# A two-layer macaron block on one core: expert biases moved out of the expert matmuls into one gate-weighted matmul per batch, second mixture in phases of 3, 3 and 2 batches, second phase's scatters close together

## What is computed

```python
x = x + 0.5 * L0_ffn(layernorm(x))     # first mixture: 8 experts, the 2 best per token
x = x + L0_attn(layernorm(x))          # 16 heads of 8, causal
x = x + 0.5 * L0_ffn(layernorm(x))     # second mixture, same weights
x = x + 0.5 * L1_ffn(layernorm(x))     # 128x128 matmul of quantized blocks, plus bias
x = x + L1_attn(layernorm(x))          # a gated scan along the sequence, then a gated FFN of 384
x = x + 0.5 * L1_ffn(layernorm(x))

# in L0_ffn, for each expert:
h = relu(x @ w1 + b1)
y = h @ w2 + b2
acc = acc + y * c[..., None]           # c: the token's gate for this expert, 0 for 6 of 8
```

## Time and profile before

| | us |
|---|---|
| median of 3 runs | 953.89 |
| lowest and highest | 950.68, 956.58 |
| the profiled execution | 953.64 |
| its span, first to last instruction | 951.9 |

### The profile page before, as it was taken

The page is one execution under the profiler, slowest core; times in us unless marked ns, Lnnn a source line. Parts: engine busy times, 40 slices in busy tenths (PEclk is TensorE's granted clock), DMA queues, the critical chain, the costliest instruction groups (busy, mean ns, idle before and its releaser), DMA issues.

```text
span 951.9 us, 23220 instructions
## 1 busy us (share of the span) xinstructions
PE 843.4 (89%) x7513; PEld 612.7 (64%) x7513; DVE 612.6 (64%) x1906; ACT 551.4 (58%) x1230; POOL 662.0 (70%) x846
## 2 busy tenths in 40 slices
PE   6379899989999999999999999999987998756894
PEld 3279798837665765665566655559965997344563
DVE  7620255674687977788979777865435335588775
ACT  4345444365568666675776667575763557735752
POOL 3789785998864378597734986971899874886432
PEclk8679899999999999998999999999999999878897
DMA  8878576736553434533443543325533771101000
GB/s 310 293 228 249 166 207 193 224 108 182 168 162 94 119 118 144 143 105 103 122 135 107 146 141 98 112 65 156 156 95 97 219 210 56 28 26 33 1 12 33
DMA packets 116280, 127.65 MB, mean 134 GB/s; under 512 B 14779, under 2 KB 84667, under 8 KB 116038
## 3 DMA queue, kind: packets, MB, share of 16 engines
q1 hardware_dynamic: 107974, 109.38, 39.4%
q0 software_dynamic: 8192, 16.79, 5.9%
HBM read 85.35 MB, written 40.39 MB: 132 GB/s over the span
## 4 chain that ended last, share of the span: by engine, by line
PE 41%; POOL 29%; DVE 15%; issue 7%; ACT 5%; DMA 2%; POOLq 0%; DVEq 0%; ACTq 0%
PE bank L801 38%; POOL z_scratch L1700 9%; POOL small L1691 9%; POOL yg L1713 4%; PE bank L813 4%; DVE sm_m L1324 3%; ACT P L1575 2%; POOL P L1735 2%; POOL sm_f L1675 1%; DMA yg<-y_scratch,pos 1%; DVE xs L1265 1%; POOL sm_p L1675 1%; DVE sm_f L1146 1%; POOL xs L1771 1%; ACT P L1488 1%
## 5 line engine op out<-in xcount | busy, mean ns | idle before, releaser
L1324 DVE TENSOR_REDUCE sm_m<-bank 128x4 f32<-128x512 f32 (+2 forms) x320 | 204.5, 683 | 37.8 <-PE bank L801 37.0
L1575 ACT ACTIVATE P<-bank 128x512 f32<-128x512 f32 x320 | 175.9, 601 | 60.1 <-PE bank L801 55.6
L801 PE MATMUL bank<-w2r,hb 128*128 x1360 | 188.0, 282 | 0.0
L801 PE MATMUL bank<-zt,wt 128*128 128x128 f32 x1360 | 182.9, 285 | 4.6 <-ACT zt L1518 2.9
L801 PEld LDWEIGHTS bank<-zt,wt 128*128 128x128 f32 x1360 | 167.3, 197 | 17.9 <-ACT P L1575 5.0
L1735 POOL TENSOR_SCALAR_AFFINE_SELECT P<-P 128x256 f32<-128x256 f32 (+1 forms) x320 | 115.5, 377 | 90.5 <-ACT P L1575 86.8
L801 PEld LDWEIGHTS bank<-w2r,hb 128*128 128x128 f32 x1360 | 165.6, 192 | 3.4 <-issue 1.6
L1700 POOL DMA_INDIRECT z_scratch<-zb,pos x128 | 134.2, 1048 | 45.7 <-issue 25.8
L1534 ACT ACTIVATE hb<-bank 128x512 f32<-128x512 f32 x170 | 101.3, 597 | 90.9 <-PE bank L801 90.5
L1691 POOL TENSOR_TENSOR small<-small 128x4 f32<-128x4 f32 x140 | 148.3, 1059 | 6.9 <-DVE pos L1247 3.6
L1713 POOL DMA_INDIRECT yg<-y_scratch,pos x128 | 130.8, 1022 | 23.9 <-issue 20.2
(11 more groups left out here) (221 smaller groups left out, 1362.5 us busy)
## 6 DMA issues: line engine op xcount, KB each, us to landing
wt<-w_scratch SPq DMA_DIRECT2D x170, 256.0 KB
zin<-z_scratch SPq DMA_DIRECT2D x82, 128.0 KB
y_scratch<-yt SPq DMA_DIRECT2D x82, 128.0 KB
q_scratch<-qpart SPq DMA_DIRECT2D x48, 128.0 KB
k_scratch<-kpart SPq DMA_DIRECT2D x48, 128.0 KB
Ks<-k_scratch SPq DMA_DIRECT2D x64, 96.0 KB
Qs<-q_scratch SPq DMA_DIRECT2D x64, 96.0 KB
z_scratch<-P SPq DMA_DIRECT2D x6, 512.0 KB, 7.0
```

Source lines behind the costliest of these rows:

```text
L801: return e.matmul(o, lhs, rhs, start=start, stop=stop, **kw)
L1324: e.tensor_reduce(to, of, AX.X, ALU.max, negate=True).then_inc(*d_max.step(i, f"m{s_}"))
L1575: e.activation(P[:, (2 * i + s_) % PR, :], shared("scor", i, 0, s_), ACT.Exp, scale=SCALE).then_inc(*a_sc.step(i, f"e{s_}"))
```

## The change

1. The expert bias leaves `res`: no `bank<-bias,ones` matmul in a block (170 fewer), and `bias` holds only the bias of L1_ffn.
2. A new stage `shift` for each of the 16 units adds `0.5 * sum(gate * b2)` to `xs` directly. DVE makes the 32 products of one-hot and gate (two operations) and their sum, PE transposes the result (128x32 to 32x128), ACT copies it out of PSUM, PE multiplies it with a block-diagonal `b2d` (32x512, a new input), and DVE adds the 512-wide result to `xs`. `comb` of a unit waits for this addition; for the second mixture the addition waits for the attention of the batch. `prep` of the next phase also waits until `share` has been computed, since it overwrites the one-hots.
3. `ORDER`: the second mixture's phases are batches 0,1,2 / 3,4,5 / 6,7 instead of 0,1 / 2,3,4 / 5,6,7. The number of blocks stays 170, in 31, 31 and 23 instead of 23, 31 and 31.
4. `apart` gives `ROWS_CLOSE` to the second phase's scatters too. Over the whole program 29 of the 140 pauses go.
5. The planner ends differently: 6 passes instead of 8, and the best pass's priorities, changed by a table `FAVOUR`, are used for one more forward pass.

The core of the diff:

```diff
-ORDER = [of(1, 0, 1), of(1, 2, 3, 4), of(1, 5, 6, 7), of(2, 0, 1), of(2, 2, 3, 4), of(2, 5, 6, 7)]
+ORDER = [of(1, 0, 1), of(1, 2, 3, 4), of(1, 5, 6, 7), of(2, 0, 1, 2), of(2, 3, 4, 5), of(2, 6, 7)]
...
-    "bias": ("D1.4 D1.4 D1.0 D1.4",
+    "bias": ("D0.4 D0.3 D0.3 D0.3",
...
-    "res": ("P1 P1+0.2 A0.3+0.15 S0.5+4.5",
+    "res": ("P0.9 P0.9+0.2 A0.3+0.15 S0.5+4.5",
...
+    "shift": ("D0.6+0.15 P0.12+0.2 A0.26+0.15 P0.45+0.2 D0.6+0.15",
+            [(1, 2), (3, 4)], 1),
...
+    if stage == "shift":
+        return [[("prep", u, 9), ("shift", u - GR, 1)], [], [("shift", u - 1, 3)], [("begin", 0, 4)],
+                [("heads", USES[u][1], 3)] if USES[u][0] == 2 else []][k]
     if stage == "comb":
-        return [("res", PAIR[last_block(OF_TILE[u])][0], 3), ("comb", u - YR, 2)] if k == 0 else []
+        return [[("res", PAIR[last_block(OF_TILE[u])][0], 3), ("comb", u - YR, 2)], [], [("shift", u // 4, 4)]][k]
...
-    return ROWS_CLOSE if stage == "scat" and OF_TILE[u] == 0 else ROWS_APART
+    return ROWS_CLOSE if stage == "scat" and OF_TILE[u] < 2 else ROWS_APART
...
+FAVOUR = {
+    "prep": {3: 5, 4: 25, 5: 25},
...
-    rows, bank_of, _ = found
+    rows, bank_of, _ = forward(plan, queues, before, {x: v + favour(x[0], x[1]) for x, v in found[1].items()})
...
+            def shift(q):
+                o = take("shift", q, 1, a_shift.at(q, "t"))
+                w.wait_ge(l_first, 64)
+                w.wait_ge(*d_shift.at(q, "g"))
+                e.transpose(o[0:32, 0:128], share[:, q % GR, 0, :], ident[:, :]).then_inc(*t_shift.step(q, "t"))
+                yield
+                o = take("shift", q, 3, d_shift.at(q, "x"))
+                w.wait_ge(l_b2, 16)
+                w.wait_ge(*a_shift.at(q, "t"))
+                mm(o, sharet[:, :], b2d[:, :], True, True).then_inc(*t_shift.step(q, "y"))
+                yield
...
-                        mm(y, ones[:, :], bias[:, bass.DynSlice(at, 128)], j == 0, False, skip_group_check=True)
                         for c in range(NC):
-                            t = mm(y, hb[u % HB][:, c, :], w2[:, bass.DynSlice(at * 4 + 128 * c, 128)], False, c == NC - 1,
+                            t = mm(y, hb[u % HB][:, c, :], w2[:, bass.DynSlice(at * 4 + 128 * c, 128)], j == 0 and c == 0, c == NC - 1,
                                    skip_group_check=True)
...
+                for k, name in enumerate("ab"):
+                    e.tensor_tensor(parts[:, k, :, :], oh[:, k, T, :], gate[:, b, k, :].unsqueeze(2).to_broadcast([128, 4, 8]), ALU.mult
+                                    ).then_inc(*d_shift.step(q, name))
+                w.wait_ge(*d_shift.at(q, "b"))
+                e.tensor_tensor(share[:, q % GR, 0, :], share[:, q % GR, 0, :], share[:, q % GR, 1, :], ALU.add
+                                ).then_inc(*d_shift.step(q, "g"))
+                yield
+                w.wait_ge(*t_shift.at(q, "y"))
+                x_ready(w, q)
+                x = xs[:, b, :, :]
+                e.tensor_tensor(x, x, blocks(shared("shift", q, 3)), ALU.add).then_inc(*d_shift.step(q, "x"))
+                yield
```

More of the change, by code:

```diff
@@ L75 @@
 SMALL = 128 + 8 * TILES
[L76 removed]
+BIAS = 128
 ZR = 5
@@ L94 @@
 YR = 5
+GR = 3
 QR = 3
@@ L273, in network @@
 def network():
-    counts = {"begin": 1, "first": 1, "xload": NB - 2, "zero": 1, "fill": 1, "late": 1, "later": 1, "sload": NE, "split": NE, "wquant": 1, "prep": 2 * NB, "route": PHASES, "scat": NTILE,
+    counts = {"begin": 1, "first": 1, "xload": NB - 2, "zero": 1, "fill": 1, "late": 1, "later": 1, "sload": NE, "split": NE, "wquant": 1, "prep": 2 * NB, "shift": 2 * NB, "route": PHASES, "scat": NTILE,
               "bias": 1,
@@ L536, in build @@
         rt = sb("rt", [128, 6, 8 * TILES])
+        share, sharet = sb("share", [128, GR, 2, 32]), sb("sharet", [32, 128])
+        b2d = sb("b2d", [32, S])
         rs = sb("rs", [128, 24 + KB + 2 * TILES + 8 * EB])
@@ L1477, in vector_program @@
             begin()
-            follow("D", {"first": first, "bias": bias_parts, "prep": prep, "route": route, "comb": comb, "proj": proj,
+            follow("D", {"first": first, "bias": bias_parts, "prep": prep, "shift": shifted, "route": route, "comb": comb, "proj": proj,
                          "maxi": maxi, "mrow": mrow, "val": val, "heads": heads, "wquant": wquant, "mxa": mx(0), "mxb": mx(1),
@@ L1505, in prep, with shift @@
                 e.activation(sm_[:, 140:144], sm_[:, 136:140], ACT.Exp).then_inc(*f.step(q, "e"))
+                yield
+            def shift(q):
+                w.wait_ge(*t_shift.at(q, "t"))
+                if q:
+                    w.wait_ge(*t_shift.at(q - 1, "y"))
+                e.activation(sharet[:, :], shared("shift", q, 1)[0:32, 0:128], ACT.Copy).then_inc(*a_shift.step(q, "t"))
                 yield
@@ L1855 @@
     w2 = g["L0_ffn_W2"].reshape(NE, NC, 128, D).transpose(2, 0, 1, 3).reshape(128, NE, 512)
-    bias = np.concatenate([g["L0_ffn_b2"].reshape(-1), g["L1_ffn_bias"]])
+    b2d = np.zeros((4, NE, 4, D), np.float32)
+    for j in range(4):
+        b2d[j, :, j, :] = g["L0_ffn_b2"]
     arrays = {
```

56 lines of the change are left out of this document (42 added, 14 removed), and 2 rows, old and new, of the table STAGES.

## The result

The changed kernel takes **968.31 us** (median), the kernel before 955.24 beside it: ratio 1.0131, 95% interval 1.0106 to 1.0157. Each of the two medians is over four executions with one far longer among them (2748.91 and 1878.18 us); the ratio leaves these two out, and the medians without them are 966.82 and 953.89. Forecast were 946.5 us and 928 to 961. By the ratio the change makes the kernel 12.5 us slower, and the result lies 6 to 7 us above the range. The profiled execution took 969.79 us.

A forecast was written before the change was run, and what follows sets the result against it. The prediction took PE as the bound from 53 to 797 us, with DVE close behind mid-kernel. Its terms, -8.2 - 3.9 - 4 - 6 + 12 + 3 = -7.1, took the profiled 953.64 us to 946.5 us, range 928 to 961.

The forecast's parts named there:

- What bounds the kernel: From 53 to 797 us PE is the bound, so work taken off it there is paid unless DVE takes over.
- The bias matmul (-18.9): In the blocks, 170 bias matmuls fewer at 0.111 us each gain 18.9 us, 10 by the lower end.
- The shift on PE (+10.7): 11 of 16 shifts, a transpose and a 0.86 us matmul each, cost PE 10.7 us; five are hidden before the first block.
- Close scatters (-3.9): Dropping 22 pauses in the second phase removes PE's exposed waits at 105 to 111 us: 3.9 us gained (2 to 6).
- The run (+12): Mid-kernel, 244 PE rows without a block take 92 us at DVE's pace against PE's 80: 12 us lost.
- It shows DVE at 95%: Sign in the profile after: DVE at 95% in the stretch of 244 PE rows without a block.
- rival D: The slow clock holds through the stretch without blocks and PE's matmuls double: 137 us against 92, 991 in all; chance 0.03.
- The border of phases 2 and 3 (+3): The stretch between the second and third phase grows from 75 to 125 rows, costing 3 us (0 to 5).
- The last phase and the tail (-4, -6): With 16 scatters and gathers instead of 24, 4 us go before the last phase's first block and 6 in the tail.
- shift and bias -8.2: The net on PE of 18.9 us gained by the bias matmuls and 10.7 us paid for the shifts.
- phases, scatters and tail +1.1: The sum's other terms: -3.9 scatters, -4 last phase, -6 tail, +12 stretch without blocks, +3 border of phases 2 and 3.
- The rival on the other side (C): The starved stretch without blocks (+21) pushes everything behind it, with gathers gaining 0: +19 in sum, 972 us; chance 0.10.

The follow-up runs named there:

- shift_only: The changed kernel planned anew with the old phases, pauses and 8 passes and an empty FAVOUR, leaving only the bias's new place: 955.37 us, ratio 1.0011.
- drop_pauses: The kernel before, order kept, without the 22 pauses among the second phase's scatters: 955.86 us, ratio 1.0018.
- fill_run: The changed kernel, order kept, with two more overwritten matmuls in each of 31 attention score steps of the long stretch without a block: 967.62 us, ratio 1.0128.
- after_again: The changed kernel measured once more, unedited, beside later experiments: 966.09 us, ratio 1.0120.
- order_only: The kernel before, planned with the new ORDER (phases of 3, 3 and 2 batches) and nothing else: 965.99 us, ratio 1.0123.
- free_gathers: The kernel before, order kept, without the 7 pauses among the last phase's gathers: 950.75 us, ratio 0.9961.
- free_end: The kernel before, order kept, without the 7 pauses among the last phase's gathers and the 13 among its scatters: 946.48 us, ratio 0.9915.
- no_favour: The whole change, planned anew with an empty FAVOUR and the 8 passes of before: 956.74 us, ratio 1.0032.
- light_reduce: The changed kernel, order kept; DVE's 62 row reductions in the long stretch without a block read a quarter of their columns: 992.19 us, ratio 1.0391.
- free_pool: The changed kernel, order kept, without POOL's 15 pauses among gathers and scatters in the long stretch without a block: 1002.07 us, ratio 1.0458.
- close_run35: The changed kernel planned anew with close scatters in all phases but the third: 1022.35 us, ratio 1.0706.
- light_shift: The changed kernel, order kept, with the shift's wide matmul and DVE's wide addition 128 columns instead of 512: 962.95 us, ratio 1.0084.
- light_both: The changed kernel, order kept, with the edits of both light_reduce and free_pool: 958.44 us, ratio 1.0033.

## Why the forecast was wrong, point by point

**What bounds the kernel.** The step that failed first is "from 53 to 797 us PE is the bound", read from busy times of 97% to 100%. Taking 170 matmuls out gave nothing, putting 170 in cost 3.4 us of the 9.4 that they take on PE.

**The bias matmul (-18.9).** The price was right (a pair of blocks falls from 4.01 to 3.79 us), the step from there to the end of the kernel was wrong: no stretch handed the time on to the end. In the last phase PE was 3.8 us ahead, and one wait that goes back to a gather took nearly all of it. Measured +2.0 us, which is nothing (interval -0.3 to +4.3). With the net of bias and shift off by 9 us, this is one of the two large misses.

**The shift on PE (+10.7).** The matmul takes 1.05 us and not 0.86; the whole shift, DVE's part included, is worth about 6 us. The net of both was forecast at -8.2; `shift_only` measured +1.1 (-0.7 to +2.8), its new plan included. That is 9 of the 20 us between forecast and result.

**Close scatters (-3.9).** They stand 1.26 us apart from 52.5 us on, as forecast, and the first block of the second phase comes sooner. But the gain did not last: `drop_pauses` shows it eaten by the next wait; in the changed kernel PE stands idle for 6.47 us for `ab` at 143.9 us, where the kernel before waits for 1.59. That step of mine asked what was exposed at one place, and not what stood ready behind it.

**The planner's end (0).** The change lists 6 passes and `FAVOUR`, and my sum gave them no price. It is the other large miss, as large as the first: the whole change with 8 passes and no table is at 1.0032, with 6 and the table at 1.0131, so 9.4 us (give or take 3). In the trace it is a run of 89 us (84.5 in the second profile) for 76, with nearly the same steps in it (705 PE records for 707, 177 of DVE for 168, 111 of POOL for 107). How much of it is the table and how much the passes is open, and so is why this order is slower.

**The run (+12).** Its length was forecast at 92 us by DVE's 88.4 at 96%; it is 84 to 89. What it costs against the same steps mixed with blocks, the +12 itself, no run measured. But the mechanism was not DVE: DVE is at 77%, the waits for `sm_m` are 1.8 us, and 21 us less of DVE's work changed nothing by itself. That the length came out near the forecast is luck: DVE alone was not the bound. "It shows DVE at 95%" was named as a sign and did not come. The clock fell further than I took it: 0.83, which is 0.34 of the time at the lower level (1.2 GHz), against 0.96 from 395 to 475 us in the kernel before. The Trainium skill (TensorE: Matmul & The Clock Gate, Part 1: The HAM clock gate) warns that the clock can fall back again and again in kernels with short waits; the trace agrees, as the run has many short waits and both levels. It did not cost what rival D put on it (137 us for the run), though what it did cost is open: `fill_run` has 0.88 and is no shorter, `after_again` has 0.90 and is 4.4 us shorter.

**The border of phases 2 and 3 (+3).** 40 us for 27, with 50 more rows in it. But this stretch grows with the shift's new plan more than with the phases: from the last `w2r,hb` before it to the first `ident,zin` behind it it is 26 us in the kernel before, 30 in `order_only` and 37 in `shift_only`, which has the old phases and loses 1.1 us in all. So most of its growth came with the shift's plan, to which the +3 gave nothing; what it costs in the changed kernel was not measured.

**The last phase and the tail (-4, -6).** 17 us were won behind the end of attention, against 10 forecast and 4 for the bias matmuls of the 36 blocks there. The direction was right, the size short of it. The likely reason is that POOL's indirect DMAs do hold the end, which `free_gathers` and `free_end` show on the kernel before; on the changed kernel it was not tested.

**In sum.** Forecast: shift and bias -8.2, phases, scatters and tail +1.1, planner's end 0. Measured by plans: +1.1 (`shift_only`), +2.0 (`no_favour` less `shift_only`), +9.4 (the planner's end): 12.5. These are differences between plans, so each holds its plan's part too. The rival on the other side (C) had the right place, a run that pushes everything behind it, and the time (972); it reached it by sizes of its own that the runs don't bear out.

## What to carry to other kernels

Before a matmul is priced at its share of a dense stretch, ask whether that stretch hands time on: leave the matmuls out with every order kept, and look at the end, not at the busy time. Where a planner writes each engine's order, an edit is two edits, the work and the new plan, and here a plan was worth more than ten microseconds; time each plan, and test the work alone with the order frozen. Taking pauses out of a queue is worth most where a chain of transfers sets the end (8.1 us for 20 of them here), and nothing where another engine's step comes next (0 for 22).

## What the runs showed of the hardware that was not expected

A float32 matmul of 512 columns with only 32 rows holds PE for 1.05 us to its follower (407.02 to 408.07 above, at a granted clock of 1.00), more than the 0.86 us of one with 128 rows, also at 1.00: fewer rows give nothing here.

A stall that stays open. In the profiles of `light_reduce`, `free_pool` and `close_run35` the first phase's blocks take 69, 71 and 78 us instead of 48, and all times of these kernels are high alike; not so in `after_again`, `fill_run`, `light_shift` and `light_both`, though `light_reduce` and `free_pool` have the same order of work as those until then. PE's and ACT's timelines of `light_reduce`:

```profile
56.02 4.77 PE L837 MATMUL bank<-zt,wt 128*128 128x128 f32 x32
...
65.13 0.60 ACT L1610 ACTIVATE hb<-bank 128x512 f32<-128x512 f32 x1 [5.50 <-remote]
71.56 0.60 ACT L1610 ACTIVATE hb<-bank 128x512 f32<-128x512 f32 x1 [5.83 <-remote]
```

And one of its stretches:

```profile
63.00:73.00 10.00, 0.19 (x1) 0.19 (x2) 1.24 (x9) 1.58 (x3) 8.09 (x9) 0.59 0.25 86
```

PE's rows for the blocks that ACT waits for end at 60.8 us, and ACT's copies of the last two start 4 and 11 us later; PE and the transfers stand still meanwhile (DMA share 0.25), and POOL's scatters go on as usual. All kernels that showed it have the close scatters at that place, and so have those that did not. `after_again` and `light_both` ran on the same chip as the three that have it, so the chip alone does not explain it. In the three the last `b2d,sharet` before the blocks starts at 52.7 to 52.9 us, in the other four at 48.6 to 49.6, so something differs before the blocks begin. What starts it was not found. It is worth 21 to 30 us, more than all parts of the change, so a comparison of whole times between edits of this kernel must first look at 53 to 125 us.
